# Attention probabilities transposed by VectorE in 32x32 blocks and a trip through DRAM, in a cross-attention and expert-FFN kernel

## The reference, cut to what matters

```python
lat = layer_norm(layernorm(x), ln_l_w, ln_l_b)
kv_in = concat([layer_norm(ctx), lat], axis=1)
sim = einsum('bhqd,bhfd->bhqf', (lat @ Wq) * scale, kv_in @ Wk)
alphas = softmax(where(mask, sim, -inf))
x = x + (einsum('bhqf,bhfv->bhqv', alphas, kv_in @ Wv) as (b, q, h*d)) @ Wo
x = x + moe_ffn(layernorm(x))
```

## Time and profile before

| | |
|---|---|
| runs, us | 1170.12, 1170.26, 1167.87; median 1170.12 |
| profiled execution, us | 1168.01 |
| its span, first to last instruction, us | 1166.3 |
| mean granted TensorE clock | 0.994 of full speed |
| busy: TensorE, VectorE, ScalarE, GpSimd | 98%, 78%, 77%, 57% |

### The profile page before, as it was taken

One profiled execution on the slowest core, in us unless ns is written; L12 is line 12 of the kernel. 1 busy time (PEld: TensorE's weight loads), 2 busy tenths in 40 slices (PEclk: granted clock), 3 DMA queues, 4 the chain that ended last, 5 costly groups with the idle time before them and its releaser, 6 DMA issues.

```text
span 1166.3 us, 29786 instructions
## 1 busy us (share of the span) xinstructions
PE 1137.6 (98%) x9000; PEld 1091.1 (94%) x9000; DVE 908.2 (78%) x4095; ACT 901.8 (77%) x3180; POOL 669.5 (57%) x781
## 2 busy tenths in 40 slices
PE   5899999999999999999999999999999999999997
PEld 5899999999999999999999999999999999999986
DVE  3778787788787788787788787788787788887776
ACT  3988788777788777788777788777788777788771
POOL 5664656665656665656565656565656565656441
PEclk8999999999999999999999999999999999999998
DMA  6001001111001111001111001111001111001101
GB/s 160 24 11 38 20 24 42 42 42 42 20 24 42 43 42 42 21 24 42 43 42 42 21 24 42 43 42 42 21 24 42 43 43 40 22 24 29 29 24 33
DMA packets 64399, 42.61 MB, mean 37 GB/s; under 512 B 8944, under 2 KB 63856, under 8 KB 64240
## 3 DMA queue, kind: packets, MB, share of 16 engines
q1 hardware_dynamic: 63056, 39.66, 12.9%
q10 hardware_dynamic: 1184, 1.05, 0.4%
HBM read 36.25 MB, written 4.45 MB: 35 GB/s over the span
## 4 chain that ended last, share of the span: by engine, by line
PE 94%; DVE 2%; issue 1%; ACT 1%; POOL 1%; DMA 1%; POOLq 0%; SPq 0%; DVEq 0%; ACTq 0%
PE bank L858 19%; PE bank L796 19%; PE bank L798 18%; PE bank L797 18%; PE bank L838 9%; PE bank L802 6%; PE bank L872 2%; PE bank L920 1%; DMA wk_raw<-in_L_xattn_Wk 1%; PE bank L909 1%; PE bank L864 1%; PE bank L779 0%; DVE MV_lo L762 0%; DVE out_sb L632 0%; ACT probs L531 0%
## 5 line engine op out<-in xcount | busy, mean ns | idle before, releaser
L430 POOL TENSOR_TENSOR probs<-probs,rdenom 128x512 f32<-128x512 f32 x256 | 266.6, 1042 | 317.4 <-DVE rdenom L662 317.4
L531 ACT ACTIVATE probs<-logits,neg_max 128x128 f32<-128x128 f32 x1024 | 402.5, 413 | 0.5 <-DVE neg_max L654 0.5
L858 PEld LDWEIGHTS bank<-kvT,tT 128*128 128x128 f32 x2048 | 267.3, 191 | 22.5
L858 PE MATMUL bank<-kvT,tT 128*128 128x128 f32 x2048 | 269.3, 274 | 0.0
L654 DVE CUSTOM_DVE_ANT_0 logits<-bank,mask_add 128x128 f32<-128x128 f32 x1024 | 232.3, 282 | 5.4 <-PE bank L858 5.1
L687 DVE TENSOR_TENSOR pT_lo<-bank,pT_hi 128x512 fp32r<-128x512 f32 x256 | 175.2, 684 | 55.1 <-ACT pT_hi L504 47.2
L531 ACT ACTIVATION_READ_ACCUMULATOR probs<-logits,neg_max 128x1 f32 x1024 | 213.5, 208 | 0.0
L504 ACT CAST pT_hi<-bank 128x512 fp32r<-128x512 f32 x256 | 152.6, 596 | 47.7 <-PE bank L838 47.2
L491 ACT ACTIVATE h_tanh<-bank 128x256 f32<-128x256 f32 x160 | 61.5, 384 | 160.9 <-PE bank L798 159.0
L697 DVE TENSOR_TENSOR cT_lo<-bank,cT_hi 128x512 fp32r<-128x512 f32 x256 | 174.7, 683 | 0.3
L796 PE MATMUL bank<-latT_hi,MV_hi 128*128 128x256 f32 x512 | 166.6, 325 | 1.9 <-DVE latT_lo L726 1.5
(11 more groups left out here) (111 smaller groups left out, 2615.4 us busy)
## 6 DMA issues: line engine op xcount, KB each, us to landing
gates<-gates_dram SPq DMA_DIRECT2D x62, 256.0 KB, 4.1
kv_raw<-in_ctx SPq DMA_DIRECT2D x32, 128.0 KB, 2.7
kv_raw<-in_x SPq DMA_DIRECT2D x32, 128.0 KB, 2.8
mask_raw<-in_mask_BxS_ik SPq DMA_DIRECT2D x32, 128.0 KB, 3.4
x_res<-in_x SPq DMA_DIRECT2D x32, 128.0 KB, 3.1
out<-out_sb SPq DMA_DIRECT2D x32, 128.0 KB, 1.8
gates_dram<-g_denseT SPq DMA_DIRECT2D x124, 2.0 KB
wv_raw<-in_L_xattn_Wv ACTq DMA_DIRECT2D x1, 512.0 KB, 5.3
```

The costliest lines, as they stand in the source:

```text
L430: nc.gpsimd.tensor_tensor(probs[n][:, :, :], probs[n][:, :, :], rdenom[n][:, :].unsqueeze(2).broadcast_to([P, PAIRS, P]), ALU.mult).then_i ...
L531: nc.scalar.activation(probs[n % 4][:, r, :], logits[n % 2][:, r, :], ACT.Exp, bias=neg_max[n % 2][:, r:r + 1], scale=-1.0, accum_out=deno ...
L858: last = nc.tensor.matmul(S_ps[k % 2][:, P * r:P * (r + 1)], tT[:, k % 4, hd:hd + 2, :], kvT[p][:, k % 4, :], start=True, stop=True)
```

## The change

The four TensorE transposes of a half, the bank they go to and the two-part split of the result are gone. Instead VectorE transposes the normalised probabilities in blocks of 32x32 (one instruction over 128x512, `probs` being laid out by key chunk, pair and key for it), SyncE stores the result to DRAM (one transfer of 256 KB) and loads it back with the blocks exchanged (four transfers of 64 KB, each to 32 partitions, in runs of 512 bytes). The value product is one float32 matmul over 512 columns from `kv_f`, of which there are three copies; steps 7 and 8 of the keys are gone, and the other six stand in halves 3 to 7 of one frame. Its two banks `C_ps` take turns. The logits are computed in half e for half e + 2 instead of e, the keys' transposes move from half 2 to half 0, and the query chunks two halves ahead. `cT` is stored by batch and read by head in runs of 32 columns. SyncE's program now goes half by half, the old transfers between the new ones: keys, mask and output in half 0, `x_res` in half 1, the gates' stores in half 5 and their loads in half 6.

```diff
-        kv_f = sb("kv_f", [P, GB, D])
-        kv_hi = [sb(f"kv_hi{n}", [P, GB, D], f32r) for n in range(2)]
-        kv_lo = [sb(f"kv_lo{n}", [P, GB, D], f32r) for n in range(2)]
+        kv_f = [sb(f"kv_f{n}", [P, GB, D]) for n in range(3)]
...
-        probs = [sb(f"probs{n}", [P, PAIRS, P]) for n in range(4)]
+        probs = [sb(f"probs{n}", [P, P // QUAD, PAIRS, QUAD]) for n in range(4)]
...
-        pT_hi = [sb(f"pT_hi{n}", [P, PAIRS * P], f32r) for n in range(2)]
-        pT_lo = [sb(f"pT_lo{n}", [P, PAIRS * P], f32r) for n in range(2)]
+        probsT = [sb(f"probsT{n}", [P, PAIRS * P]) for n in range(2)]
+        probsT_dram = [nc.dram_tensor(f"probsT_dram{n}", [P, PAIRS * P], fp32, kind="Internal").ap() for n in range(3)]
+        pT = [sb(f"pT{n}", [P, PAIRS * P]) for n in range(3)]
...
-        cT_hi = [sb(f"cT_hi{n}", [P, H, GB, S], f32r) for n in range(2)]
-        cT_lo = [sb(f"cT_lo{n}", [P, H, GB, S], f32r) for n in range(2)]
+        cT_hi = [sb(f"cT_hi{n}", [P, GB, 2, PAIRS * P], f32r) for n in range(2)]
+        cT_lo = [sb(f"cT_lo{n}", [P, GB, 2, PAIRS * P], f32r) for n in range(2)]
...
-        PT_ps, C_ps, T_ps, WY_ps, H_ps, X_ps = banks[1:7]
+        T_ps, WY_ps, H_ps, X_ps = banks[3:7]
+        C_ps = (banks[1], banks[2])
...
+            ahead = 1 if k >= 1 else 0
+            return ((k + 7) % HALVES, ahead) if has(j, p, -ahead, NG - 1 - ahead) else None
...
+        def head_columns(cT, hd):
+            hh, r, odd = hd // 8, hd % 8 // 2, hd % 2
+            return cT.rearrange("p b t (o a r q) -> p b t o a r q", o=2, a=2, r=PAIRS)[:, :, hh, odd, :, r, :]
...
+            def store_probs(s):
+                n = s % 3
+                sp.wait_ge(probsT_ready, s + 1)
+                after(sp, pT_loaded[n], 64 * (s // 3))
+                sp.dma_start(probsT_dram[n], probsT[s % 2][:, :]).then_inc(probsT_stored[n], 16)
+            def load_probs(s):
+                n = s % 3
+                sp.wait_ge(probsT_stored[n], 16 * (s // 3 + 1))
+                after(sp, C_in_psum, s - 2)
+                for c in range(P // QUAD):
+                    sp.dma_start(pT[n][QUAD * c:QUAD * (c + 1), :].rearrange("k (a f) -> k a f", a=P // QUAD),
+                                 probsT_dram[n].rearrange("(a k) (c f) -> c k a f", a=P // QUAD, c=P // QUAD)[c]
+                                 ).then_inc(pT_loaded[n], 16)
...
+                for k in range(HALVES):
+                    e = HALVES * i + k
+                    if has_half(e - 1):
+                        store_probs(e - 1)
+                    if has_half(e - 2):
+                        load_probs(e - 2)
+                    if k == 0 and has(j, p, -1, NG - 3):
+                        load_kv(j, p + 2)
+                        load_mask(j, p + 2)
+                    if k == 0 and has(j, p, 4, NG + 2):
+                        store_out(i - 1)
+                    if k == 1 and has(j, p, 0, NG - 1):
+                        after(sp, x1_step, 3 * (i - 2) + 1)
+                        sp.dma_start(x_res[p][:, :, :],
+                                     x.rearrange("b s d -> (b s) d")[bass.ds(GT * i, GT), :].rearrange("(t q) d -> q t d", q=P)
+                                     ).then_inc(x_res_loaded[p], 16)
+                    if k == 5 and has(j, p, 2, NG):
+                        sp.wait_ge(gate_step, GATE_STEPS * (i - 1))
+                        after(sp, gates_loaded, 32 * (i - 2))
+                        for a in range(P // QUAD):
+                            sp.dma_start(gates_dram.rearrange("e (t a q) -> e t a q", t=TT, a=P // QUAD)[:, :, a, :],
+                                         g_denseT[QUAD * a:QUAD * a + E, :, :]).then_inc(gates_stored, 16)
+                    if k == 6 and has(j, p, 2, NG):
+                        sp.wait_ge(gates_stored, 64 * (i - 1))
+                        after(sp, h_routed_done, NT * (i - 2))
+                        for a in range(2):
+                            sp.dma_start(gates[FH * a:FH * (a + 1), :, :],
+                                         gates_dram.rearrange("(r a) t -> a r t", a=2)[a, :, :].partition_broadcast(FH)
+                                         ).then_inc(gates_loaded, 16)
+                if i == NG + 2:
+                    store_out(i)
+            def store_out(i):
+                after(sp, out_ready, i - 2)
+                sp.dma_start(out.rearrange("b s d -> (b s) d")[bass.ds(GT * (i - 3), GT), :].rearrange("(t q) d -> q t d", q=P),
+                             out_sb[(i - 1) % 2][:, :, :]).then_inc(out_stored[(i - 1) % 2], 16)
...
+                    after(pool, C_in_psum, HALVES * (g - 2))
+                    nc.gpsimd.tensor_tensor(kv_f[g % 3][:, :, :], kv_n[:, :, :],
                                             ln_b_bc[:, :].unsqueeze(1).broadcast_to([P, GB, D]), ALU.add).then_inc(kv_step, 1)
-                if 7 in steps:
-                    after(pool, C_in_psum, HALVES * (g - 1))
-                    pool.wait_ge(kv_step, step + 6)
-                    nc.gpsimd.tensor_copy(kv_hi[par][:, :, :], kv_f[:, :, :]).then_inc(kv_step, 1)
-                if 8 in steps:
-                    pool.wait_ge(kv_step, step + 7)
-                    nc.gpsimd.tensor_tensor(kv_lo[par][:, :, :], kv_f[:, :, :], kv_hi[par][:, :, :].bitcast(fp32),
-                                            ALU.subtract).then_inc(kv_step, 1)
...
-                    if has_half(j, p, k, 2):
-                        n = (k - 2) % 4
-                        pool.wait_ge(rdenom_ready, e - 1)
-                        nc.gpsimd.tensor_tensor(probs[n][:, :, :], probs[n][:, :, :],
-                                                rdenom[n][:, :].unsqueeze(2).broadcast_to([P, PAIRS, P]),
+                    if has_half(e):
+                        n = e % 4
+                        pool.wait_ge(rdenom_ready, e + 1)
+                        by_pair = probs[n][:, :, :, :].rearrange("p c r k -> p r c k")
+                        nc.gpsimd.tensor_tensor(by_pair, by_pair,
+                                                rdenom[n][:, :].unsqueeze(2).unsqueeze(3).broadcast_to([P, PAIRS, P // QUAD, QUAD]),
                                                 ALU.mult).then_inc(probs_ready, 1)
...
-                    if has(j, p, -1, NG - 2):
-                        keys(j, p + 1, {0: (5,), 1: (6,), 4: (7,), 5: (8,)}.get(k, ()))
                     if has(j, p, -2, NG - 3):
-                        keys(j, p + 2, {5: (1, 2), 6: (3,), 7: (4,)}.get(k, ()))
+                        keys(j, p + 2, {3: (1, 2), 4: (3,), 5: (4,), 6: (5,), 7: (6,)}.get(k, ()))
...
-                    if has_half(j, p, k, 3):
-                        n = (k - 3) % 2
-                        act.wait_ge(pT_in_psum, e - 2)
-                        after(act, C_in_psum, e - 4)
-                        nc.scalar.copy(pT_hi[n][:, :], PT_ps[:, :]).then_inc(pT_hi_ready, 1)
-                    if has_half(j, p, k, 4):
-                        kl, par = half_buffers(p, k, 4)
-                        act.wait_ge(C_in_psum, e - 3)
+                    if has_half(e - 4):
+                        c = e - 4
+                        g, kl = c // HALVES, c % HALVES
+                        act.wait_ge(C_in_psum, c + 1)
                         if kl == 0:
-                            after(act, W_in_psum, i - 1)
-                        nc.scalar.copy(cT_hi[par][:, 8 * (kl // 4):8 * (kl // 4) + 8, kl % 4, :],
-                                       C_ps[:, :].rearrange("p (h q) -> p h q", h=8)).then_inc(cT_hi_ready, 1)
+                            after(act, W_in_psum, g - 1)
+                        nc.scalar.copy(cT_hi[g % 2][:, kl % 4, kl // 4, :], C_ps[c % 2][:, :]).then_inc(cT_hi_ready, 1)
...
+                    if has_half(e + 1):
+                        c = e + 1
+                        for r in range(PAIRS):
+                            act.wait_ge(logits_ready, PAIRS * c + r + 1)
+                            if r == 0:
+                                after(act, probsT_ready, c - 3)
+                            nc.scalar.activation(probs[c % 4][:, :, r, :], logits[c % 2][:, r, :].rearrange("p (c k) -> p c k", k=QUAD),
+                                                 ACT.Exp, bias=neg_max[c % 2][:, r:r + 1], scale=-1.0,
+                                                 accum_out=denom[c % 4][:, r:r + 1]).then_inc(exp_done, 1)
...
+                    if has_half(e + 1):
+                        c = e + 1
+                        g, kl = c // HALVES, c % HALVES
+                        dve.wait_ge(S_in_psum, c + 1)
                         if kl == 0:
-                            dve.wait_ge(mask_ready, i + 1)
-                        after(dve, exp_done, PAIRS * (e - 2))
+                            dve.wait_ge(mask_ready, g + 1)
+                        after(dve, exp_done, PAIRS * (c - 1))
                         for r in range(PAIRS):
                             nc.vector.tensor_tensor_reduce(
```

(83 more changed lines are left out.)

93 lines of the change are left out of this document (23 added, 70 removed).

## The result

The changed kernel takes 1157.64 us, median of six runs (1153.85 to 1161.72); the kernel before 1168.21 in six runs beside it. The ratio is 0.9904, 95% interval 0.988 to 0.9929: about 1% faster, 10.6 us where 46 were forecast. The profiled execution of the changed kernel took 1153.85 us (span 1152.1), 3.8 us under its median.

A forecast was written before the change was run, and what follows sets the result against it. TensorE, busy 98%, was taken as the bound: 33.0 us a frame plus 0.6 of stall make 33.6, 1.43 less than 35.03; over 32 frames 46 us less, 1168 - 46 = 1122 us, range 1080 to 1182.

The forecast's parts named there:

- the likeliest mechanism: TensorE at 33.0 us a frame, stalls of 0 to 1.2 from late loads: 1103 to 1141 us, chance 0.52.
- Rival 3: Float32 product costs its low end: TensorE needs 29.7 us a frame, the queue then sets 1077 us; chance 0.13.
- the three orders: New waits: transposed keys' copy-out before `x2`, VectorE's transpose behind GpSimd, gates' transfers behind probabilities; claimed to cost nothing while covered.
- Rival 4: VectorE's transpose at its upper bound and GpSimd late, so the product waits: about 1168 us, no change; chance 0.04.
- 4*0.65 + 0.45 = 3.05 per half: SyncE's issue time for four loads at 0.65 us and one store at 0.45; 24.4 us a frame.
- rival 1: SyncE's queue sets a slower end: dear load issues and stores, 36.1 us a frame, 1202 us; chance 0.19.
- rival 2: SyncE's queue takes back most of the gain: load pitch 0.69, 1141 us, or 1157 with landing waits; chance 0.12.
- The sign set for rivals 1 and 2: TensorE waiting on `pT` over 1 us a frame, with SyncE issuing without a gap.
- the signs for the forecast: Two product records 0.4 us apart, transpose near 0.70, loads every 0.65, TensorE over 96% busy, short waits in halves 0 to 3.
- The 0.6: Stall charged per frame in us: gates' loads delay the store behind them by some 0.8, 3.1 against 2.5.
- 2.5 to spare: Slack in us between loads and product after issue and a 2.7 landing, if the transpose is done when TensorE begins its half.
- 2*33.0/8 = 8.25 us cover: Loads issued in half s+2, product at s+4: two halves cover 0.45 + 2.6 of issue and a 2.7 landing.

The follow-up runs named there:

- the kernel without the trip: Changed kernel without the store to DRAM and the loads back; the product reads VectorE's blocks where they lie, unsorted: 1097.8 us, ratio 0.9403.
- Split and spread together: Changed kernel, output, keys, mask and `x_res` moved to halves 2 to 4, gates' stores in halves 5 and 6, loads in 7 and 0: 1111.17 us, 0.9503.
- the kernel with a lag of five and no trip: Changed kernel with product five halves behind its logits, projection heads moved, no store or loads of the probabilities: 1140.67 us, ratio 0.9759.

## Why the prediction was right and wrong

The direction held, and the likeliest mechanism with it: TensorE gets shorter, the trip through the queue takes part of it back by late loads in a few halves. The size did not: 35 us were missing.

**TensorE: right, slightly low.** The product took 0.86 us where 0.89 was taken from the logits' row; a frame without the trip is 32.82 where 33.0 was forecast. Over 32 frames that is 2.2 * 32 = 71 us, and the kernel without the trip is 71.9 below the kernel before. Rival 3, the cheap product, is out: the two records are one kind of pass of 0.43 us. By the rule of four passes in the Trainium skill (FP8 and Floating Point Precision, TensorE Precision Notes) the estimate was 0.93; the trace gives 0.86, so rule and row are near each other here.

**VectorE, ScalarE, GpSimd, the three orders: right.** VectorE's transpose took 0.688 against 0.70, the normalisation 1.041 as before in spite of its pattern, and the kernel without the trip shows no new wait of any weight. Rival 4 is out.

**SyncE's issue: too dear.** The step "4*0.65 + 0.45 = 3.05 per half" took 64-partition rows for 32-partition loads. Four loads take 1.82 (0.455 each) and the store 0.34 to 0.41, so a half needs about 2.3, and the frame 8*2.3 + 7.2 = some 26 us, not 31.4. The queue never set the pace, and rival 1 with its pitch of 0.72 is out. So is the mechanism of rival 2, whose time of 1157 us was met by chance: the queue gaps show in SyncE's 189.7 us of waits for VectorE. The sign set for rivals 1 and 2, waits of over 1 us a frame, did come (1.20), but not what was to go with it, a SyncE that issues without a gap. Of the signs for the forecast, short waits in halves 0 to 3 came; TensorE was busy 94%, not over 96%.

**The stall: the step that failed.** The forecast charged 0.6 us a frame, 19 in all; the trip cost 59.8. A frame lost 34.37 - 32.82 = 1.55 us, or 50 over 32 frames. The 0.6 were those of half 7, whose loads are issued in half 1, where the lag was to be largest (2.3 and 0.8 against 2.5 to spare); half 7 waits 0.27 a frame. For half 5, whose loads are issued in half 7, the forecast had 2.0 of lag against the same 2.5 to spare, so no stall; half 5 waits 0.83. What failed is "2*33.0/8 = 8.25 us cover", which takes all halves as equally long.

They are not. TensorE's products in the changed kernel:

```profile
655.83 1.02 PE L860 MATMUL bank<-pT,kv_f 128*128 128x512 f32 x2
660.74 1.02 PE L860 MATMUL bank<-pT,kv_f 128*128 128x512 f32 x2
663.21 1.02 PE L860 MATMUL bank<-pT,kv_f 128*128 128x512 f32 x2
666.84 1.02 PE L860 MATMUL bank<-pT,kv_f 128*128 128x512 f32 x2
```

Half 7 starts at 660.74, half 0 at 663.21, half 1 at 666.84: half 5's loads have 6.10 us from the start of half 7 to their product, not 8.25. The forecast's 2.5 us to spare are 0.35; with its own lag of 2.0 that is a stall of 1.65 us, where the one shown above cost 1.55. The kernel before showed it already; TensorE's transposes there, the two neighbours of the one in the earlier trace rows:

```profile
600.58 0.60 PE L838 MATMUL bank<-ident,probs 128*128 128x128 f32 x4
...
606.77 0.60 PE L838 MATMUL bank<-ident,probs 128*128 128x128 f32 x4
```

Two halves in a row last 6.19 us together. (For half 7 the cover was as forecast: its two halves, 1 and 2, last 8.65 at the median.)

The way from the queue to the product was no longer than forecast. At the median of the 26 frames SyncE is 1.54 us late at half 7, needs 2.58 to issue half 6's store and half 5's loads, and the last load has landed 2.77 after that: 6.89, where the forecast had 2.0 + 3.05 + 2.7 = 7.75. So the landing was priced rightly for the loads that matter, though the median load lands 2.2 us after its issue begins. Behind the end of the last issue it takes 1.6 in halves 1 to 4 and 6, and 2.77 in half 5 and 2.37 in half 7, which stand behind bursts. Pieces of the chain (start, us), ahead of the late products at 608.42 (half 7's) and 805.05 (half 5's):

```profile
593.47 4.26 DMA probsT_dram<-probsT
...
604.40 3.98 DMA pT<-probsT_dram
...
796.88 1.38 SPq L335
...
801.84 3.17 DMA pT<-probsT_dram
```

A store behind the gates' loads took 4.26 us to land, a load behind keys, mask, output and a store 3.98. The late product of the stretch above adds up so: 2.47 of lag, 2.57 of issue (799.74 to 802.31) and 2.74 until the product at 805.05 make 7.78, where the two halves gave 805.05 - 1.29 - 797.27 = 6.49; the difference is the 1.29 of the wait. Its lag is above the median because one load's issue took 1.38 us, where 0.43 is the median. Of the 1024 loads' issues 34 take over 0.7 us, in nearly every half; the runs do not show why.

The sum, with what the runs give: TensorE 72 instead of 64 us gained, the trip 60 instead of 19 lost, which is 33 of the 35 us.

**The end: charged at nothing.** Between the profiled executions the trip costs 1152.1 - 1095.6 = 56.5 us (the other 3.3 of the 59.8 are there because the changed kernel's profiled execution lies 3.8 under its median). Of these, 50 are 32 frames at 1.55, and 6.9 lie behind the last of VectorE's transposes: from there to the end of the span it is 1152.1 - 1107.09 = 45.0 us in the changed kernel, against 1095.6 - 1057.55 = 38.1 without the trip. There two products wait 1.88 and 3.09 us:

```profile
1106.57 1.50 PE L860 MATMUL bank<-pT,kv_f 128*128 128x512 f32 x2 [1.88 <-DMA pT<-probsT_dram]
1112.44 2.07 PE L860 MATMUL bank<-pT,kv_f 128*128 128x512 f32 x2 [3.09 <-DMA pT<-probsT_dram]
```

That TensorE has less other work ahead of them there is likely, but was not tried.

**Issue time against a rule.** The Trainium skill (DMA: Bandwidth & Descriptors, Issuing engines are not separate DMA queues) calls the time to start a DMA usually small beside the DMA. By it the time would have been 1103. Here one issue of 0.455 us is a fifth of its landing of 2.2, so the sentence fits a single transfer; but four in a row take 1.82, and three gates' stores fewer in a frame are worth 33 us. For a queue with five transfers in every half the issues could not be left out. That five issues are longer than any one landing was too strong: the gates' loads take 4.1 us to land, and five issues take 2.3 here, about as long as one landing of `pT`. The forecast was right to price them, and took them too dear.

**What stays open.** Of the 1.55 us that a frame loses, the product's waits show 1.20; the 31 waits in 26 frames, each with the 0.26 that the stall above cost beyond its wait, make another 0.31. Split and spread together are still 13 us above the kernel without the trip. Between the profiled executions (spans 1109.8 and 1095.6) 7.8 of the difference lie before VectorE's transpose of half 24, where TensorE waits 6.6 us for loads, most of it at the first four products; 2.5 lie in the 26 frames, and 3.8 behind the last transpose, where two products wait 0.28 and 2.71. Whether those waits can be taken away was not tried, nor why an issue now and then takes 1 us longer.

## What to carry to other kernels

Price an in-order DMA queue at its worst point, not by its sum: take the shortest stretch that the product's lead can be, subtract every issue that stands ahead of the load there, and use the landing behind the burst that stands there (2.77 us here against 1.6). Moving one burst only moves the stall to where the next burst stands; all of them have to be broken up at once (1164.77 and 1147.26 us alone, 1111.17 together). A longer lag also buys the time, but then look at what the moved work was covering.

## What was not expected of the hardware

Issue time depends on the transfer: 0.455 us for a load to 32 partitions, against 0.64 to 64 partitions in the earlier trace rows. It also depends on what stands ahead. The mask took 0.60 behind the keys, and in the kernel with spread and split, where it follows loads of `pT` instead, 0.43:

```profile
630.96 0.43 SPq L304 DMA_DIRECT2D mask_raw<-in_mask_BxS_ik  x1
```

TensorE's clock fell in the tail. Stretches of the changed kernel's tail (length, busy PE, PEld, DVE, ACT, POOL, granted clock, DMA share, GB/s):

```profile
1104.00:1107.00 3.00, 1.12 (x3) 0.30 (x2) 1.88 (x6) 0.59 (x1) 0.00 (x0) 1.00 0.54 161
1107.00:1110.00 3.00, 2.35 (x8) 1.44 (x6) 1.46 (x4) 0.59 (x1) 2.29 (x5) 0.53 0.97 269
1110.00:1113.00 3.00, 0.56 (x1) 0.50 (x2) 0.00 (x0) 0.00 (x0) 2.64 (x4) 0.50 0.62 183
1113.00:1116.00 3.00, 3.00 (x10) 1.85 (x8) 0.83 (x2) 1.14 (x3) 0.00 (x0) 0.50 0.55 155
```

a stretch in its middle:

```profile
600.00:672.00 72.00, 69.90 (x510) 61.51 (x509) 60.13 (x267) 51.81 (x195) 39.38 (x46) 1.00 0.53 159
```

and the tail of the kernel without the trip:

```profile
1057.55:1070.00 12.45, 9.81 (x62) 7.60 (x62) 7.99 (x24) 3.64 (x9) 4.90 (x8) 1.00 0.01 1
```

After the wait of 1.88 us, in which TensorE was busy 1.12 of 3 us, the granted clock was 0.50 to 0.53 (1.2 GHz) until about 1120, where the other kernel kept 1.00 (2.4 GHz). The product's records there last 1.50 and 2.07 us instead of 1.02. A late load is not needed for that: in the kernel with a lag of five and no trip, which has no such loads, the clock fell in the tail too, after a stretch with TensorE busy 0.93 of 3 us:

```profile
1097.00:1100.00 3.00, 0.93 (x2) 0.10 (x1) 2.52 (x8) 0.58 (x1) 1.91 (x4) 1.00 0.00 0
...
1103.00:1106.00 3.00, 3.00 (x10) 1.97 (x9) 0.84 (x2) 0.38 (x1) 0.00 (x0) 0.50 0.00 0
```

So a late load in the tail cost its wait, and TensorE ran slower after it; the waits of 0.85 and 1.25 us in the middle stretch, at 608.42 and 642.60, left the clock at 1.00. How much of the 6.9 us at the end comes from the clock was not measured.
